# Issuing the restack's loads from SP's queue in place of ACT's, and moving the wait that guards them

## The reference, cut to what matters

```python
perm = (logits == jnp.max(logits, axis=-3, keepdims=True)).astype(x.dtype)
permuted = jnp.einsum('bntd,bntes->bnesd', grouped, perm)
inner = jax.nn.relu(jnp.einsum('bnesd,esdf->bnesf', permuted, W1) + b1)
result_permuted = jnp.einsum('bnesf,esdf->bnesd', inner, W2) + b2
result = jnp.einsum('bnesd,bntes->bntd', result_permuted, perm)
```

## Time and profile before

| | |
|---|---|
| time, median of 3 runs | 4903.62 us (4897.01 to 4905.12) |
| time of the profiled execution | 4904.44 us |
| span of its slowest core (core 5) | 4902.9 us |
| spans of the 8 cores | 4861.7 to 4902.9 us |
| PE busy | 2597.5 us (53%) |
| DVE busy | 1497.7 us (31%) |
| ACT busy | 1836.4 us (37%) |

### The profile page before, as it was taken

One profiled execution on the slowest core, in us unless ns is written; L12 is line 12 of the kernel. 1 busy time (PEld: TensorE's weight loads), 2 busy tenths in 40 slices (PEclk: granted clock), 3 DMA queues, 4 the chain that ended last, 5 costly groups with the idle time before them and its releaser, 6 DMA issues.

```text
span 4902.9 us, 64777 instructions; the slowest of 8 cores (4861.7 to 4902.9 us)
## 1 busy us (share of the span) xinstructions
PE 2597.5 (53%) x19792; PEld 1411.4 (29%) x19792; DVE 1497.7 (31%) x3689; ACT 1836.4 (37%) x3808; POOL 18.2 (0%) x35
## 2 busy tenths in 40 slices
PE   4666745433376665554346666463336666645441
PEld 1333324311133332432123333242113333334210
DVE  1322134322332113543233221443233222144332
ACT  0355633211324564331034556333122455533213
POOL 0000000000000000000000000000000000000000
PEclk9668766555677887555576788665557678856555
DMA  4200052377400001027731000104752000010574
GB/s 88 61 18 18 1 112 70 73 134 159 120 35 26 6 14 61 35 57 141 134 102 44 18 18 1 61 36 87 165 110 99 18 18 18 9 52 36 132 140 124
DMA packets 174812, 324.86 MB, mean 66 GB/s; under 512 B 5654, under 2 KB 136982, under 8 KB 168986
## 3 DMA queue, kind: packets, MB, share of 16 engines
q10 hardware_dynamic: 140224, 117.45, 11.7%
q1 hardware_dynamic: 26330, 163.94, 11.4%
q0 software_dynamic: 7936, 39.33, 4.8%
HBM read 239.95 MB, written 120.07 MB: 73 GB/s over the span
## 4 chain that ended last, share of the span: by engine, by line
PE 40%; ACT 19%; DMA 18%; issue 10%; DVE 10%; ACTq 1%; SPq 0%; DVEq 0%; POOL 0%; POOLq 0%
PE pp_pv L398 8%; DMA rpe<-rp_scratch 8%; DMA rp_scratch<-rpn 8%; ACT pT L374 7%; PE pp_s L366 6%; PE pp_w L475 6%; PE pp_s L303 5%; PE pp_s L677 4%; PE pp_s L646 3%; PE pp_s L729 2%; ACT x2b L635 2%; ACT pTn L420 2%; DVE pT L382 2%; PE pp_pv L729 2%; DVE x L483 2%
## 5 line engine op out<-in xcount | busy, mean ns | idle before, releaser
L374 ACT ACTIVATE pT<-pp_s,c_negC 128x512 bf16<-128x512 f32 x1280 | 845.8, 691 | 354.2 <-PE pp_pv L398 210.0
L398 PE MATMUL pp_pv<-vS,pT 128*128 128x129 bf16 x5120 | 620.4, 258 | 390.4 <-DVE pT L382 229.0
L398 PEld LDWEIGHTS pp_pv<-vS,pT 128*128 128x128 bf16 x5120 | 393.7, 112 | 795.8 <-issue 792.8
L366 PE MATMUL pp_s<-qT,kT 128*128 128x512 bf16 x1280 | 600.0, 487 | 0.1
L382 DVE TENSOR_TENSOR pT<-pT,c_zl 128x512 bf16<-128x512 bf16 x512 | 217.7, 425 | 957.7 <-ACT pT L374 957.5
L729 PE MATMUL pp_s<-w_2t,inr 32*64 32x256 bf16 x1024 | 146.0, 402 | 594.9 <-DVE rpn L742 492.3
L303 PE MATMUL pp_s<-xT,w_q 128*128 128x512 bf16 x1024 | 229.4, 388 | 283.4 <-DMA w_kv<-cwkv 214.3
L742 ACT CAST rpn<-pp_s 128x256 bf16<-128x256 f32 x256 | 95.4, 373 | 727.0 <-DMA rpe<-rp_scratch 654.4
L475 PE MATMUL pp_w<-w_o,atT 128*128 128x512 bf16 x1024 | 273.0, 427 | 94.0 <-DVE x L483 80.0
L742 DVE CAST rpn<-pp_s 128x256 bf16<-128x256 f32 x256 | 108.7, 425 | 613.3 <-DMA rpe<-rp_scratch 560.9
L646 PE MATMUL pp_s<-pmt,x2b 32*128 32x128 bf16 x1024 | 127.5, 280 | 269.3 <-ACT x2b L635 259.2
(11 more groups left out here) (86 smaller groups left out, 2872.9 us busy)
## 6 DMA issues: line engine op xcount, KB each, us to landing
rp_scratch<-rpn SPq DMA_DIRECT2D x32, 2048.0 KB, 18.1
rpe<-rp_scratch ACTq DMA_DIRECT2D x32, 2048.0 KB, 24.3
xtile<-x SPq DMA_DIRECT2D x64, 512.0 KB, 3.8
y<-x SPq DMA_DIRECT2D x64, 512.0 KB, 5.7
w<-cw ACTq DMA_DIRECT2D x12, 2048.0 KB, 7.9
w_2t<-cw ACTq DMA_DIRECT2D x48, 512.0 KB, 12.0
xT<-xT POOLq DMA_DIRECT2D x4, 4096.0 KB, 26.7
w<-w POOLq DMA_DIRECT2D x4, 2048.0 KB, 16.8
```

The costliest lines, as they stand in the source:

```text
L366: return inc("tensor", "sPE", 1, lambda e, kc=kc, ping=ping, h=h, qb=qb: e.matmul(pp_s[ping][:, :], kT[:, kc * 128: kc * 128 + 128], qT[:, ...
L374: ev = inc("scalar", "sACT", 1, lambda e, ping=ping: e.activation(out=pT[ping][:, :], in_=pp_s[ping][:, :], func=AF.Exp, bias=c_negC, scal ...
L398: ping=ping, sub=sub, kc=kc, kcmax=kcmax: e.matmul(bank[:, colo: colo + 129], pT[ping][:, sub * 128: sub * 128 + 128], vS[:, kc * 132: kc ...
```

## The change

The guard `("rpe",)` is waited for by SP in place of ACT, ahead of SP's 64 waits. The two loads of the restack, and the waits for the stores ahead of them, stand on SP's list in place of ACT's.

```diff
         def emit_restack(q4):
-            gwait("scalar", ("rpe",))
+            gwait("sync", ("rpe",))
             for mm_ in rsq_all[q4]:
                 wait("sync", mm_)
             for hh in range(2):
                 sth = inc("sync", ["sRSa", "sRSb"][hh], 16, lambda e, hh=hh: e.dma_start(
                     out=bass.AP(drp.tensor, drp.offset + 64 * hh * 16384,
                                 [[16384, 64], [1, 16384]]),
                     in_=rpn[64 * hh: 64 * hh + 64, :]))
-                wait("scalar", sth)
-                inc("scalar", "sRS", 16, lambda e, hh=hh: e.dma_start(
+                wait("sync", sth)
+                inc("sync", "sRS", 16, lambda e, hh=hh: e.dma_start(
                     out=rpe[64 * hh: 64 * hh + 64, :].rearrange("p (g d) -> p g d", d=256),
                     in_=bass.AP(drp.tensor, drp.offset + 64 * hh * 16384,
                                 [[256, 64], [16384, NG], [1, 256]])))
```

## The result

The changed kernel takes 5036.14 us (median of 10 runs) against 4905.22 us of the kernel before in the same job: a ratio of 1.0269, 95% interval 1.0242 to 1.0295, which is 131 us slower (119 to 145). The forecast was 5103 us with a range of 5015 to 5165. The direction was as forecast, and so were the delay of the stores and what it gives back; the size was two thirds of it, and the experiments say which term was too large.

The account below looks back on a forecast made before the run. No engine was busy throughout; whatever lengthens or delays a restack, a store-then-load DMA round trip, was taken to go on the end one for one. 110 + 36 + 88 - 35 = 199 us on 4904 gave 5103 us, range 5015 to 5165.

Parts of the forecast that it names:

- Part 1: In ten restacks SP waits for the previous quarter's scatter before the stores, starting them 11.0 us later: 110 us.
- Part 2: After the guard SP must still pass 64 already met waits, 3.6 us in each of ten restacks: 36 us.
- Part 3: Each restack's four transfers in a row on one queue take 50.5 us against 45.0: 16 x 5.5 = 88 us.
- the forecast's lower bound: For the four transfers in a row: 46.5 us a restack, +1.5, or 24 us in all.
- Part 4: Later stores avoid the W2 load behind e2(1) and e2(2): six restacks 5.9 us shorter, -35 us.
- What costs nothing: ACT losing two waits and two issues, SP holding them, and PE's longer wait at its clock level add no time.
- The queue does not matter: Rival: engines take what they have, four transfers in a row cost 0 to 2 us a restack: 5015 to 5047 us; chance 0.14.
- The long start of a load: Rival: a load has its own start latency, needing 22.4 us each, +22.3 a restack: 5372 us; chance 0.06.
- the quick load: Rival: a load alone on the engines takes 7.9 us, 6.7 less a restack: 4908 us; chance 0.03.
- the hidden guard: Rival: PE ends the scatter before SP sees the last copy, leaving only 88 us: 4992 us; chance 0.04.

Follow-up runs that it names:

- The order alone: Changed kernel with the guard moved behind store 0, loads still on SP in the changed order: 4911.21 us against 4901.24 of the kernel before, ratio 1.003.
- The guard alone: Kernel before with the guard on SP ahead of its 64 waits, loads left on ACT: 5052.27 us, timed again 5027.94 against 4909.88, ratio 1.0255.
- The queue alone: Kernel before with SP issuing everything in the old order, both stores, guard, then loads: 4904.16 us against 4909.88, ratio 1.0009.
- one at a time: Changed kernel with SP also waiting for each load to land before issuing what follows: 5146.66 us against 4901.24 of the kernel before, ratio 1.0485.
- padding: Kernel before with 4 KB of padding behind each 32 KB row of the scratch tensor: 4903.07 us against 4909.88, ratio 0.998.
- store 1 on the other queue: Changed kernel with store 1 issued from ACT's queue: 5056.53 us against 4899.5 of the kernel before, ratio 1.0299.

## Why the prediction was right, and where it was too large

**Part 1, the guard ahead of the stores: right.** Forecast 10 x 11.0 us. The run with the guard behind the waits has its stores 11.3 us behind the last copy, 0.1 before, in the ten restacks that were named; the six others did not move. 112 us.

**Part 2, the 64 waits: right.** Forecast 10 x 3.6. Measured 14.7 - 11.3 = 3.4, 34 us by the traces, 26 us by the ratios and 33 by the medians. The row of the first sequence was the right place to read it, since there the waits were passed already met.

**Part 3, four transfers in a row: the term that was mis-sized.** The step was "Store 1 queued behind load 0 lands at 12.0 + 1.1 + 12.2 + 10.6 = 35.9". It lands at 31.5. Load 0 lands at 26.2, 0.9 later than its share of that sum, and load 1 alone takes 14.4 us (forecast 14.6, though no row gave the 13.5 in it); wrong was the 10.6 us for store 1, taken from a store behind a store. Behind a load it costs 5.3. The DMA queue of the changed kernel over 8 us of store 0 and over 4 us that hold the end of load 0 and three quarters of store 1, from 2433 and from 2456 (the GB/s are by slices of 0.2 and of 0.1 us):

```profile
GB/s 328 0 0 0 0 0 0 0 0 0 0 819 1638 164 0 0 0 0 0 0 0 0 0 0 1475 1147 0 0 0 0 0 0 0 0 0 0 0 1802 819 0
...
q1 hardware_dynamic: 50, 1.64, 99.7%
...
GB/s 497 799 778 1403 722 56 374 41 358 364 666 0 0 0 0 328 655 328 1638 655 328 328 328 328 328 0 0 328 328 655 1311 983 328 328 328 328 328 0 0 0
...
q1 hardware_dynamic: 223, 1.65, 111.9%
```

The same 1.6 MB take half the time. The last quarter of store 1 doesn't share in this; the window 2460.1:2463.2 holds its 16 packets of 32 KB (and 16 of under 512 bytes):

```profile
DMA packets 32, 0.52 MB, mean 169 GB/s; under 512 B 16, under 2 KB 16, under 8 KB 16
...
q1 hardware_dynamic: 32, 0.52, 77.6%
```

That is 0.776 x 3.1 = 2.4 us a packet, nearly the 2.56 of store 0. The other part of the gain is overlap: store 1's first packets move from 2456.0 on (the window 2455:2456 has none of over 2 KB), 2.0 us ahead of load 0's landing (2443.7 + 14.3 = 2458.0). A row of the kernel before held a warning that a store alone is no measure of what the DMA can do: beside the W2 load it moved 282 GB/s in all, where stores alone move 205. So a restack cost 1.4 us more (2.0 beside a W2 load) and not 5.5: 24 us in all, where 88 was taken. That 24 is also the forecast's lower bound is luck: the bound came from loads of 12.0 us and a store of 10.45 us, and measured were 14.3 and 5.3. The 64 us between them are nearly all of the 67 us from 5103 to the measured 5036. The order alone, at +15 us (2 to 27), agrees.

**Part 4, the collision with the W2 load: right.** Forecast 6 x -5.9. The six restacks run at 46.3 us, which with the 1.4 of part 3 is -5.5 each, -33 us. The guard alone shows them at 45.0.

**What costs nothing: right.** The queue alone made no difference.

112 + 34 + 24 - 33 = 137 us by the parts, 131 (119 to 145) by the clock.

**The rivals.** "The queue does not matter" gave 5015 to 5047 us and holds the measured 5036, which lies under the range of 5050 to 5150 that the forecast gave itself, with a chance of 0.72 against 0.14 for this rival: the stated range of 5015 to 5165 holds it because it was drawn to take in this rival. Its mechanism is half true: the queue is worth nothing (1.0009), but the order on it is not, since each transfer in a row does pay its start and end, and part of that is given back by the quick store. The long start of a load (22.4 us each) is excluded by the 14.3 us of a load alone; the quick load (7.9 us) by the same number; the hidden guard by the 14.7 us.

**Open.** Why a 32 KB store packet takes 2.56 us behind a store or alone, and about half of that for three quarters of a store behind a load in the same queue, is not settled. It isn't the half of the partitions (one at a time: 11.9 for both), not the row pitch (padding), and a load that only waits in the other queue doesn't quicken it (store 1 on the other queue: 12.0). Nor does it take a load in the same queue: the kernel before had quick packets too, where its first store moved beside the W2 load on ACT's queue (restack(1) of the second sequence, window 2250.6:2256.4):

```profile
q1 hardware_dynamic: 48, 1.57, 73.5%
q10 hardware_dynamic: 127, 0.48, 32.0%
```

That is 0.735 x 5.8 x 16 / 48 = 1.4 us a packet. What goes with the difference in these traces is how the 16 engines stand to each other: in the slow window under part 3 they take up their packets together, with none taken up in between, and in the quick one the packets are spread over the slices. Whether that is the cause was not tested; no run here puts the engines in or out of step by itself.

## What to carry to other kernels

When a wait moves to another engine's list, price what stands behind it there and not the wait: here one line put 11 us of hidden work, and 64 small waits, in front of a round trip, ten times over. Put a wait that is met late behind the ones that are met early. A transfer's price taken where it stands behind one kind of neighbour need not hold behind another: here it was 10 us and 5. A long transfer between two stages is shortened by starting its first part beside the stage ahead, as long as nothing that must land early stands behind something slow in the same queue.

## What the runs showed of the hardware

- The time for a 2 MB store depended on what stood ahead in the same queue: 11.9 us alone, 10 more behind a store, 5.3 more behind a load of 512-byte rows. Its 32 KB packets took 2.56 us each while all 16 engines took them up in step (alone, behind a store), and about half of that in the first three quarters of the store behind the load and beside the W2 load (1.4 us).
- A load of 512-byte packets on one queue all but stood still beside a store of 32 KB packets on the other: 32 packets against 64 in 10 us, none in the first 6 us and then turn by turn.
- 64 waits that are already met cost SP 3.4 to 3.6 us, some 55 ns each.
- An issue can hold its engine: 7.5 us for a store issued behind a load, 10.8 us for one behind four.
